# A Mamba scan regrouped: four channels by 32 states in a group, instead of 128 channels by one state

## The reference, cut to what matters

```python
xz = jnp.einsum('bld,ed->ble', x, W_in)
xc, z = jnp.split(xz, 2, axis=-1)
xp = jnp.pad(xc, ((0, 0), (D_CONV - 1, 0), (0, 0)))
xconv = sum((xp[:, k:k + Ls, :] * conv_w[:, k] for k in range(D_CONV))) + conv_b
u = jax.nn.silu(xconv)
dbc = jnp.einsum('bld,ed->ble', u, W_xproj)
dt_lo = dbc[..., :DT_RANK]
Bm = dbc[..., DT_RANK:DT_RANK + D_STATE]
Cm = dbc[..., DT_RANK + D_STATE:]
dt = jax.nn.softplus(jnp.einsum('blr,dr->bld', dt_lo, W_dt) + b_dt)
A = -jnp.exp(A_log)
def step(h, t):
    dt_t, B_t, C_t, u_t = t
    h = h * jnp.exp(dt_t[:, :, None] * A) + (dt_t * u_t)[:, :, None] * B_t[:, None, :]
    y = jnp.einsum('bds,bs->bd', h, C_t)
    return (h, y)
_, ys = jax.lax.scan(step, h0, xs)
y = ys.transpose(1, 0, 2) + u * D
y = y * jax.nn.silu(z)
return jnp.einsum('bld,ed->ble', y, W_out)
```

## Time and profile before

| What | Value |
|---|---|
| median of 3 executions | 1231.24 us (1227.08 to 1231.66) |
| the profiled execution, its own time | 1228.37 us |
| its span, first to last instruction | 1226.5 us |
| mean granted TensorE clock | 0.864 of full speed |
| busy over the span | TensorE 899.4 us, VectorE 888.0, ScalarE 629.2, GpSimd 485.4 |

### The profile page before, as it was taken

One profiled execution on the slowest core, in us unless ns is written; L12 is line 12 of the kernel. 1 busy time (PEld: TensorE's weight loads), 2 busy tenths in 40 slices (PEclk: granted clock), 3 DMA queues, 4 the chain that ended last, 5 costly groups with the idle time before them and its releaser, 6 DMA issues.

```text
span 1226.5 us, 13379 instructions
## 1 busy us (share of the span) xinstructions
PE 899.4 (73%) x3453; PEld 517.9 (42%) x3453; DVE 888.0 (72%) x1124; ACT 629.2 (51%) x1060; POOL 485.4 (40%) x392
## 2 busy tenths in 40 slices
PE   4784076577757999684068788878888888888788
PEld 2342034556625665342024344434443444444466
DVE  0234989865442222666989999999999999996365
ACT  0255131174362444465367666766776667663631
POOL 0002557620200000001367767776777677762100
PEclk9897587686576999887579999999999999999876
DMA  9600000700100000000000000000000000000001
GB/s 231 135 0 0 0 1 0 151 1 1 52 1 0 1 1 1 0 1 0 0 1 1 0 1 1 1 0 1 0 1 0 0 1 0 1 0 1 1 14 25
DMA packets 14416, 19.11 MB, mean 16 GB/s; under 512 B 5534, under 2 KB 13726, under 8 KB 13854
## 3 DMA queue, kind: packets, MB, share of 16 engines
q1 hardware_dynamic: 14366, 18.51, 6.8%
HBM read 17.31 MB, written 1.20 MB: 15 GB/s over the span
## 4 chain that ended last, share of the span: by engine, by line
DVE 36%; PE 32%; issue 14%; ACT 9%; POOL 3%; SPq 2%; DMA 2%; DVEq 1%; ACTq 0%; POOLq 0%
DVE pair_arrays L1421 15%; DVE PS L1408 6%; ACT pair_arrays L789 5%; PE PS L527 3%; PE PS L536 3%; PE PS L552 2%; PE PS L734 2%; PE PS L620 2%; PE PS L463 2%; DMA big<-in_x 2%; POOL pair_arrays L1117 2%; PE PS L760 2%; PE PS L434 1%; PE PS L628 1%; DVE pair_arrays L1223 1%
## 5 line engine op out<-in xcount | busy, mean ns | idle before, releaser
L1117 POOL TENSOR_TENSOR pair_arrays<-pair_arrays 128x736 f32<-128x736 f32 x192 | 335.6, 1748 | 54.8 <-DVE pair_arrays L1421 53.4
L628 PE MATMUL PS<-pair_arrays,weights 128*128 128x368 f32 x768 | 305.2, 480 | 0.2 <-POOL pair_arrays L1117 0.2
L789 ACT ACTIVATE pair_arrays<-PS 128x736 f32<-128x736 f32 (+6 forms) x246 | 176.7, 721 | 212.9 <-PE PS L620 152.3
L620 PE MATMUL PS<-pair_arrays,token_weights 128*128 128x368 bf16 x768 | 186.7, 326 | 124.3 <-DVE pair_arrays L1421 88.2
L1421 DVE TENSOR_TENSOR_SCAN pair_arrays<-pair_arrays,scan_carry,PS 128x368 f32<-128x368 f32 x256 | 240.3, 988 | 0.0
L789 ACT ACTIVATE pair_arrays<-big,A_negative 128x368 f32<-128x368 f32 x384 | 207.8, 591 | 0.0
L620 PEld LDWEIGHTS PS<-pair_arrays,token_weights 128*128 (+1 forms) x768 | 71.2, 98 | 306.5 <-issue 209.4
L1408 DVE TENSOR_TENSOR PS<-big,PS 128x736 f32<-128x736 f32 x192 | 178.6, 930 | 3.0 <-POOL big L1104 2.5
L628 PEld LDWEIGHTS PS<-pair_arrays,weights 128*128 128x128 f32 x768 | 126.5, 190 | 20.4 <-POOL pair_arrays L1117 1.3
L1069 POOL TENSOR_TENSOR big<-pair_arrays 128x1104 f32<-128x1104 f32 (+15 forms) x32 | 59.4, 1873 | 149.2 <-DVE pair_arrays L1177 114.9
L1421 DVE TENSOR_TENSOR_SCAN pair_arrays<-pair_arrays,PS 128x368 f32<-128x368 f32 x128 | 112.3, 922 | 1.0 <-ACT pair_arrays L789 1.0
(11 more groups left out here) (190 smaller groups left out, 1282.3 us busy)
## 6 DMA issues: line engine op xcount, KB each, us to landing
big<-in_x SPq DMA_DIRECT2D x8, 1024.0 KB, 19.4
big<-decay_rows SPq DMA_DIRECT2D x4, 1104.0 KB, 15.1
weights<-in_wts SPq DMA_DIRECT2D x1, 1949.5 KB, 20.7
big<-in_wexp SPq DMA_DIRECT2D x1, 1536.0 KB, 7.6
out_h<-big SPq DMA_DIRECT2D x8, 128.0 KB
pair_arrays<-in_wdft SPq DMA_DIRECT2D x1, 696.0 KB, 3.8
txt_rows<-in_txt SPq DMA_DIRECT2D x1, 77.0 KB
out_h<-big SPq DMA_DIRECT2D x1, 77.0 KB
```

Of the source, the lines that this page charges most:

```text
L620: last = nc.tensor.matmul(PS[:, bank + h, 0:G], pick[:, bass.ds((n * (2 * NPS) + (2 * c + h)) * 128, 128)], SBC[:, kind, seg * G:(seg + 1) ...
L628: last = nc.tensor.matmul(PS[:, seg % 2, 0:G], w("ident"), hcbuf[c][:, h, :], start=False, stop=stop, skip_group_check=True)
L789: return nc.scalar.activation(o, i, fn, **kw)
L1117: nc.gpsimd.tensor_tensor(hcbuf[c], hbuf[c], cbuf[c], ALU.mult).then_inc(s("hc_ready"), 1)
```

## The change

- A group is now 4 channels by 32 states: a partition is one channel and one state. A step covers two groups, 8 channels, and a segment again has 16 steps. Segments run piece by piece over the four batches, where they ran batch by batch; `carry` has 128 columns.
- B and C are projected with weights that repeat the 32 states four times, so their projections are already laid out as the scan needs them; they are kept in f32 as `B4` and `C4` and are no longer spread in the scan.
- What is spread in the scan is dt and dt*u: per step and operand two f32 matmuls with contraction 32 (partitions r to r+31) that write 128 partitions. dt*u goes to banks 2 and 3, dt to banks 4 and 5 or 6 and 7. Each group's rows lie in another quarter of the partitions; the two halves of dt*u are stored swapped, so that the four spreads of a step read four different quarters.
- y is gathered with f32 matmuls of contraction 128 that write 32 partitions each (`ysel`), the additions of two steps together, every second step.
- The decays are made in place in PSUM; VectorE's product goes to SBUF (`bx`); the scan reads the decays from PSUM and `bx` from SBUF. ScalarE copies nothing in the scan. All loops are unrolled.
- Before the scan, the convolution is folded into the projection: four taps, each an f32 matmul with contraction 64, for the two batches of a pair in the two halves of the partitions. dt, B and C are evacuated once. The softplus goes piece by piece over all four batches, its series by a Square on ScalarE; GpSimd has no part in it.

```diff
-           ("Win", 4 * DI), ("XB", 128), ("XC", 128), ("XD", 128), ("WdtT", DI), ("WoutT", 2 * 128), ("FF1", 128),
+           ("Win", 2 * DI), ("XB", 128), ("XC", 128), ("XD", 128), ("WdtT", DI), ("WoutT", 2 * 128), ("FF1", 128),
...
-           ("conv_w", KC), ("cols", 16)]
+           ("cwrow", KC * DI), ("ysel", NQ * DB), ("cols", 17)]
...
+            def in_proj(u):
+                k, p = u // NPAIR, u % NPAIR
+                bank = 4 * (u % 2)
+                pe.wait_ge(s("ln_out"), 2 * NGR + p * NG + k + 1)
+                pe.wait_ge(s("ln_ln"), 3 * NGR)
+                if u >= 2:
+                    pe.wait_ge(s("u_ready"), u - 1)
+                    pe.wait_ge(s("z_ev"), u - 1)
+                for j in reversed(range(KC)):
+                    back = KC - 1 - j
+                    skip = back if k == 0 else 0
+                    for b2 in range(2):
+                        last = nc.tensor.matmul(PS[:, bank + b2, skip:G], win_tap[64 * b2:64 * b2 + 64, j * DI:(j + 1) * DI],
+                                                P1[64 * b2:64 * b2 + 64, p, k * G + skip - back:(k + 1) * G - back],
+                                                start=(back == 0), stop=(j == 0))
+                last.then_inc(s("xc_ps"), 1)
...
+            def low_rank(u):
+                bank = 4 * (u % 2)
...
+                if u >= 2:
+                    pe.wait_ge(s("dt_abs"), u - 1)
+                    pe.wait_ge(s("dt_relu"), u - 1)
+                    pe.wait_ge(s("c_ev"), u - 1)
+                for b2 in range(2):
+                    last = nc.tensor.matmul(PS[:, bank + b2, 0:G], w("XD"), u_of(u, b2), start=True, stop=True)
+                last.then_inc(s("dlo_ps"), 1)
+                for b2 in range(2):
+                    last = nc.tensor.matmul(PS[:, bank + 2 + b2, 0:G], w("XB"), u_of(u, b2), start=True, stop=True)
+                last.then_inc(s("b_ps"), 1)
+            def steps_of(u):
+                bank = 4 * (u % 2)
+                pe.wait_ge(s("dlo_ev"), u + 1)
+                for b2 in range(2):
+                    last = nc.tensor.matmul(PS[:, bank + b2, 0:G], w("WdtT"), dlo[u % 2][:, b2, :], start=True, stop=True)
+                last.then_inc(s("dt_ps"), 1)
+                pe.wait_ge(s("b_ev"), u + 1)
+                for b2 in range(2):
+                    last = nc.tensor.matmul(PS[:, bank + 2 + b2, 0:G], w("XC"), u_of(u, b2), start=True, stop=True)
+                last.then_inc(s("c_ps"), 1)
+            for u in range(NPAIR * NG):
+                low_rank(u)
+                if u:
+                    steps_of(u - 1)
+            steps_of(NPAIR * NG - 1)
...
+            def spread_input(t):
+                seg, i = t // NSTEP, t % NSTEP
+                if i == 0:
+                    pe.wait_ge(s("dt_ready"), seg // B + 1)
+                if t:
+                    pe.wait_ge(s("b_used"), t)
+                for h in range(2):
+                    r = DB * ((2 * (i % 2) + h + 2) % 4)
+                    last = nc.tensor.matmul(PS[:, 2 + h, 0:G], pick[r:r + DB, (i // 2) * 128:(i // 2 + 1) * 128],
+                                            at(2, seg)[r:r + DB], start=True, stop=True)
+                last.then_inc(s("x_spread"), 1)
+            def spread_step(t):
+                seg, i = t // NSTEP, t % NSTEP
+                if t >= 2:
+                    pe.wait_ge(s("scanned"), 2 * (t - 1))
+                for h in range(2):
+                    r = DB * (2 * (i % 2) + h)
+                    last = nc.tensor.matmul(PS[:, 4 + 2 * (t % 2) + h, 0:G], pick[r:r + DB, (i // 2) * 128:(i // 2 + 1) * 128],
+                                            at(1, seg)[r:r + DB], start=True, stop=True)
+                last.then_inc(s("dt_spread"), 1)
+            def add_y(t):
+                seg, i = t // NSTEP, t % NSTEP
+                if i == 0:
+                    start_y(seg)
+                pe.wait_ge(s("hc_ready"), t + 1)
+                for h in range(2):
+                    r = DB * (2 * (i % 2) + h)
+                    last = nc.tensor.matmul(PS[r:r + DB, seg % 2, 0:G], w("ysel")[:, (i // 2) * DB:(i // 2 + 1) * DB],
+                                            hcbuf[t % NRING][:, h, :], start=False, stop=(i == NSTEP - 1 and h == 1),
+                                            skip_group_check=True)
+                last.then_inc(s("y_added"), 1)
+            for t in range(NSEG * NSTEP):
+                spread_input(t)
+                spread_step(t)
+                if t % 2 == 0 and t >= 4:
+                    add_y(t - 4)
+                    add_y(t - 3)
...
+            for u in range(NPAIR * NG + 1):
+                if u < NPAIR * NG:
+                    left(u)
+                if u >= 1:
+                    magnitude(u - 1)
+                    if u % 2 == 0:
+                        logarithms(u // 2 - 1)
+                        square(u // 2 - 1)
+            def decay(t):
+                act.wait_ge(s("dt_spread"), t + 1)
+                for h in range(2):
+                    f(PS[:, bank, 0:G], PS[:, bank, 0:G], ACT.Exp, scale=aneg[:, g:g + 1]).then_inc(s("decay"), 1)
...
+            for u in range(NPAIR * NG):
+                evacuate(u)
+                if u % 2:
+                    softplus(u // 2)
+            def input_term(t):
+                dve.wait_ge(s("x_spread"), t + 1)
+                tt(bx[t % NRING], b4(seg).unsqueeze(1).to_broadcast([128, 2, G]), PS[:, 2:4, 0:G], ALU.mult).then_inc(s("b_used"), 1)
+            for t in range(NSEG * NSTEP):
+                if t:
+                    scan_half(t - 1, 0)
+                input_term(t)
+                if t:
+                    scan_half(t - 1, 1)
+                if t % NSTEP == 6 and t >= NSTEP:
+                    finish_y(t // NSTEP - 1)
```

More of the change, by code:

```diff
@@ L196, in ring @@
[L196 to L202, removed]
+        def ring(i):
+            n = 2 * NRING * G
+            return [work[:, i * n:(i + 1) * n].rearrange("p (c h t) -> p c h t", c=NRING, h=2)[:, c] for c in range(NRING)]
@@ new lines, in _ @@
+            pe.wait_ge(s("win_ready"), 1)
+            def in_proj(u):
[15 more added lines that the diff above has]
+                for b2 in range(2):
+                    last = nc.tensor.matmul(PS[:, bank + 2 + b2, 0:G], w("Win")[64 * b2:64 * b2 + 64, DI:2 * DI],
+                                            P1[64 * b2:64 * b2 + 64, p, cols(k)], start=True, stop=True)
+                last.then_inc(s("z_ps"), 1)
@@ L999, in _, with pair_cols @@
-            for seg in range(NSEG):
-                step_act(seg, 0, True)
-                with act.Fori(1, NS) as n:
-                    step_act(seg, n, False)
+            def pair_cols(i, u):
+                return pair_of(i, u % NPAIR)[:, :, cols(u // NPAIR)]
+            for u in range(NPAIR * NG):
+                bank = 4 * (u % 2)
+                act.wait_ge(s("xc_ps"), u + 1)
+                f(pair_cols(0, u), PS[:, bank:bank + 2, 0:G], ACT.Silu, bias=col("conv_b")).then_inc(s("u_ready"), 1)
+                act.wait_ge(s("z_ps"), u + 1)
+                f(pair_cols(3, u), PS[:, bank + 2:bank + 4, 0:G], ACT.Silu).then_inc(s("z_ev"), 1)
@@ new lines, in magnitude, with logarithms @@
+            def magnitude(u):
+                bank, p, k = 4 * (u % 2), u % NPAIR, u // NPAIR
+                act.wait_ge(s("dt_ps"), u + 1)
+                if k >= 2:
+                    act.wait_ge(s("dt_series"), k - 1)
+                f(soft(0, k)[:, 2 * p:2 * p + 2, :], PS[:, bank:bank + 2, 0:G], ACT.Abs, bias=col("b_dt")).then_inc(s("dt_abs"), 1)
+            def logarithms(k):
+                act.wait_ge(s("dt_abs"), NPAIR * (k + 1))
+                f(soft(0, k), soft(0, k), ACT.Exp, scale=-1.0).then_inc(s("dt_exp"), 1)
+                act.wait_ge(s("dt_exp"), k + 1)
+                if k:
+                    act.wait_ge(s("dt_sum"), k)
+                f(soft(2, k), soft(0, k), ACT.Ln, bias=ONE).then_inc(s("dt_log"), 1)
@@ L1125, in _ @@
+            for t in range(NSEG * NSTEP):
+                output_term(t)
+            pool.wait_ge(s("x_spread"), NSTEP * NSEG)
+            pool.wait_ge(s("dt_spread"), NSTEP * NSEG)
             nc.gpsimd.memset(later[:, 128:SP], 1.0)
@@ L1425, in step_dve @@
-            def step_dve(seg, n, before, number=None):
-                early = number == 0 and seg == 0
-                for c in range(NPS):
-                    last = (seg, n, c - 1) if c else (*before, NPS - 1) if before is not None else None
-                    last_early = early if c else number == 1 and seg == 0
-                    if last is not None:
-                        scan_half(*last, 0, last_early)
-                    input_term(seg, n, c)
-                    if last is not None:
-                        scan_half(*last, 1, last_early)
+                        dve.wait_ge(s("carried"), t - B * NSTEP + 1)
```

378 lines of the change are left out of this document (123 added, 255 removed).

## The result

| | Before | After |
|---|---|---|
| median | 1230.24 us (1227.08 to 1231.66, 4 executions) | 1314.22 us (1311.99 to 1316.31, 4 executions) |
| ratio, 95% interval | | 1.0675 (1.0647 to 1.0703): slower |
| profiled span | 1226.5 us | 1313.1 us |
| mean granted TensorE clock | 0.864 | 0.678 |

What follows compares the result with a forecast made beforehand. VectorE was taken to bound the scan before the change. Profiled span 1226.5 + 57.5 (scan) - 38.2 (stage before) + 1.1 (weights) + 2 (cold start) = 1248.9, 1250.8 with 1.9 around it; execution 2.9 below median, so 1254 us, range 1188 to 1278.

Steps and rivals of the forecast that it cites:

- TensorE, at full clock there: Scan: TensorE was taken to run at full clock, a f32 matmul costing 0.617 us, two passes of 0.309.
- 2 us for a cold start: Start of the scan: TensorE, idle for some 12 us before, begins at half clock, +2 us.
- the loop's terms: Scan, waits over two steps: step spread 0.93, additions 1.54, input spread 0.93 and others, 5.49 us, 5.55 with carry.
- In-order passes overlap: Scan, main case: matmuls on different array parts start passes in order, n taking n + 1 passes; scan +57.5 us, chance 0.45.
- the three ends: TensorE's price in the scan: nothing overlaps (7.40 us in two steps), everything in another part overlaps, or in-order passes overlap.
- everything in another part of the array overlaps: Scan, one possible price for TensorE: 0.617 us for each group of two or four matmuls.
- the favourable rival: Scan: groups overlap whole, the loop takes 3.95 us, TensorE never holds VectorE up; 1196 us, chance 0.37.
- a group of four additions spanning about 1.5 us: Scan: a mark set down as showing in-order passes; a span of 0.6 would show whole overlap, 2.5 none.
- The stage before the scan: From the norm's last passes to the scan's first product: first product at 580.2 instead of 618.36, -38.2 us.
- The tiling change: TensorE in the scan: changing between tilings costs 0.12 us once in two steps, ends 0 and 0.28; 11.5 us.
- What I costed at nothing: Scan: VectorE's product writing SBUF, its scan reading decays from PSUM, and ScalarE's decays in PSUM add no time.
- The stage after: Behind the scan: the same as before the change, difference 0.

Runs made afterwards that it cites:

- Runs 1: Changed kernel plus two idle f32 matmuls of 128 rows in every two steps, left out at segment changes: 1210.5 us, ratio to before 0.9829.
- run 2: Changed kernel plus two idle matmuls in every two steps that read only 32 rows: 1290.84 us, one execution.
- run 6: Changed kernel plus two idle matmuls of 128 rows in every two steps, at segment changes too: 1200.79 us, ratio to before 0.9761.
- runs 9: Changed kernel without idle matmuls, the odd steps' dt spreads given selectors of 128 rows, zero outside their 32: 1204.74 us, ratio to before 0.9794.
- run 10: The kernel of run 6 with one idle matmul in place of two: 1200.86 us, one execution.
- run 8: Kernel before the change, its two additions of a step made over 32 rows instead of 128: 1615.31 us, one execution.
- run 3: Changed kernel plus three idle matmuls of 128 rows in every two steps: 1221.27 us, ratio to before 0.9927.
- run 7: The kernel of run 6 plus twelve idle matmuls of 128 rows after the scan's first two spreads: 1208.09 us, ratio to before 0.9819.
- run 5: Changed kernel plus two idle matmuls of 128 rows in every two steps that write only 32 columns: 1212.57 us, one execution.

## Why the prediction was wrong

**The step that failed: "TensorE, at full clock there".** It was read off, where the clock is 0.99, and carried into a scan whose matmuls had been changed from 128 rows to 32 for eight in twelve. Apart from 2 us for a cold start no term, bound or rival of the forecast held the clock of the scan open, though the granted clock varied between stages in the rows at hand (0.50, 0.74, 0.99). Runs 1, 2, 6, 9 and 10 show it: wide matmuls bring the clock back, idle ones or the scan's own, and with it 104 to 113 us; the same matmuls with 32 rows bring back 23. In the kernel before, narrow additions keep the clock at half (run 8), there together with the changes of tiling. At half clock the loop's terms were 1.52, 1.39 and 1.64 where 0.93, 1.54 and about 1.1 (0.93 with latency) stood, and 6.42 in all against 5.55 (5.67 with the change of tiling).

**A second step failed the other way: "In-order passes overlap".** Whole groups overlap. In the projection eight matmuls on two halves take 2.47 us from start to start (503.86 to 506.33), that is four times 0.617; the rule of n + 1 passes wanted 2.78. Of the three ends, "everything in another part of the array overlaps" was the true one. The Trainium skill, "TensorE: Matmul & The Clock Gate", section "Part 3: Packing small matmuls — row/col tiling", has small matmuls on different tiles start 4 ns apart; the records of L664 and L675 agree as far as they resolve it (806.66 and 806.67), for f32 matmuls of two passes too. I had let the two records of one matmul, one after the other, speak against it, but those are on the same part and say nothing of another part.

**So the favourable rival was right in its mechanism.** It gave 1196; with the clock held up the kernels measured 1200.8 and 1200.9. The forecast of a loss got its sign from a mechanism that isn't there, and the loss came from one that it didn't name. One of the marks that I had set down would have misled: "a group of four additions spanning about 1.5 us" reads 1.46 here, but that is two passes at half clock, and 0.83 at full. The waits for the input spread are there too, though longer (1.2 us on average, not 0.4 to 0.7), and the pairs are 6.4 us apart and not 5.5 to 5.7. A duration proves a mechanism only beside the clock of its stretch.

**The stage before the scan:** right, -36.1 against -38.2. The projections ended at 519.4, where 520.1 was expected: a unit took 3.09 us instead of 3.39, since the halves overlap wholly, but the first began at 499.10 instead of 497.8. The chain behind them took 64 us where I had 60.1. The clock, 0.77 there, may be part of that; no run parts it.

**The tiling change:** the 0.12 us once in two steps was of the right order at full clock (800.00 to 800.87 is 0.87, two passes of 0.309 are 0.62, so 0.25 with what the input spread waits for itself); at half clock it is 0.16 (1.39 less 1.23), in run 8 0.29 from narrow f32 to bf16 of 128 rows and 0.11 back. The Trainium skill, "TensorEngine Tiling (Array Packing)", section "Key Properties", has a change of mode drain TensorE; these rows agree with a small price for it.

**What I costed at nothing** held: product 0.92, recurrences 0.97 and 0.91 us, decays 0.54 in PSUM. The weights' DMA and the start cost 1.2 us (forecast 1.1). **The stage after** cost 2.3 us that I had at 0. The output projection's first group takes 5.26 us at half clock, where it took 2.74; but in run 6, behind a scan at full clock, it takes 5.22, so the scan's level is not the reason. And where the code of this stage is the same the time behind the scan varies from 107.0 us (run 3) to 121.6 (run 7), so that 2.3 us say little.

**Left open.** What in the changed kernel's mix lets the clock fall, when four of its twelve matmuls already have 128 rows: the runs show that wide matmuls added or widened bring it back, and no more. A count of wide matmuls does not explain it: in run 8 four of the six matmuls of a step have 128 rows, in bf16, and the clock stays at half, while in run 10 one wide f32 matmul more in two steps is enough. Nor does the work of the moment decide alone, since run 2 keeps either level with the same loop. Whether the type (f32 or bf16) matters was not tried. Why the kernels with added work reach the first product 0 to 6 us later than the changed kernel (583.48 in run 5, 589.67 in run 7, against 583.45): the difference is there by VectorE's first copy out of PSUM after the projections (526.92 in the changed kernel, 530.84 in run 6), from where all of them take 56.5 to 56.7 us. Idle matmuls were not tried in the chain ahead of the scan other than in run 7.

## What to carry to other kernels

When an edit cuts matmuls into tiles of 32 rows, ask what the granted clock will be afterwards, not only how well the tiles overlap: here they overlapped better than forecast, and nearly every matmul of the stage took twice as long. Read the clock of each stretch first, in stretches short enough to see its two levels, and price TensorE at both. If it falls, make a few of the stage's own matmuls use all 128 rows with zeros, or put one idle wide matmul where the engine waits: here that turned 6.8% slower into 2.1% and 2.3% faster (runs 9 and 10).

## What the runs showed of the hardware

- Mean granted clock by mix in the scan: 0.53 to 0.56 with eight f32 matmuls of 32 rows and four of 128 x 32 in two steps; 0.60 to 0.81 with two more of 32 rows, which is stretches of up to 38 us at 1.00 and up to 58 us at 0.50 with the same loop; 0.94 with two of 128 rows by 32 columns instead, 0.97 with two of 128 x 128; 1.00 once no segment change lacked them, and with one as with two. The four additions of 128 rows that the changed kernel has were not enough by themselves.
- Separate row tiles that overlap in time, four quarters at once (806.66), together reach all 128 rows, and the clock stayed at half all the same.
- The kernel before, at 100% busy with f32 matmuls of 32 rows between bf16 ones of 128 (run 8), stays at 0.50 for all of the 300 us shown. A TensorE without a gap is not enough for the full clock.
- f32 matmuls on different quarters or halves overlap in both passes: eight on two halves 2.47 us, four on four column quarters 0.83 us with latency (1.46 at half clock).
